# Two unweighted graph layers computed with a dense matrix of edge counts instead of a gather at each edge step

## What is computed

```python
h = relu(_layernorm(x)); x = x + relu(segment_sum((h @ W0)[src] * edge_weight, dst))
h = relu(_layernorm(x)); x = x + relu(segment_sum(norm * (h @ W1.T + b)[src_or_loop], dst_or_loop))
h = relu(_layernorm(x)); x = x + (relu((h + segment_sum(h[src], dst)) @ G1 + g1) @ G2 + g2)
h = relu(_layernorm(x)); x = x + attention over the edges with 8 heads (segment softmax, segment sum)
```

## Time and profile before

| | us |
|---|---|
| three runs | 3065.06, 3089.04, 3067.91; median 3067.91 |
| span of the profiled execution | 3090.3 |
| PE busy, PEld busy | 2381.9 (77%), 1214.8 (39%) |
| DVE, ACT, POOL busy | 1594.0 (52%), 329.1 (11%), 1792.2 (58%) |
| DMA | 557 MB, mean 180 GB/s |
| POOL's gathers of table rows into `ring` | 1721, of some 0.96 us each |

### The profile page before, as it was taken

One profiled execution on the slowest core, in us unless ns is written; L12 is line 12 of the kernel. 1 busy time (PEld: TensorE's weight loads), 2 busy tenths in 40 slices (PEclk: granted clock), 3 DMA queues, 4 the chain that ended last, 5 costly groups with the idle time before them and its releaser, 6 DMA issues.

```text
span 3090.3 us, 32287 instructions
## 1 busy us (share of the span) xinstructions
PE 2381.9 (77%) x8238; PEld 1214.8 (39%) x8238; DVE 1594.0 (52%) x3866; ACT 329.1 (11%) x496; POOL 1792.2 (58%) x1878
## 2 busy tenths in 40 slices
PE   7888888887668777775778888785068598887886
PEld 5444444433223222221344555453058443333332
DVE  8755555644234443323244444444058467777666
ACT  5200000000000000000000000001068200000000
POOL 0466666665566666665666666653710456666665
PEclk9899999998789989887889999997579789999989
DMA  6676666675567766666666666662134457676665
GB/s 161 199 227 175 181 178 179 195 232 164 170 177 212 205 195 209 190 191 183 182 195 198 201 198 199 193 198 69 14 107 146 140 168 206 204 230 191 191 193 163
DMA packets 212803, 557.09 MB, mean 180 GB/s; under 512 B 55477, under 2 KB 56878, under 8 KB 212645
## 3 DMA queue, kind: packets, MB, share of 16 engines
q0 software_dynamic: 144448, 462.60, 52.2%
q1 hardware_dynamic: 67514, 91.15, 9.5%
q10 hardware_dynamic: 683, 1.28, 0.2%
HBM read 515.28 MB, written 39.59 MB: 180 GB/s over the span
## 4 chain that ended last, share of the span: by engine, by line
PE 53%; DVE 13%; issue 13%; another core or an unknown queue 11%; DMA 6%; POOL 3%; ACT 0%; SPq 0%; DVEq 0%; POOLq 0%; ACTq 0%
PE tiles L1520 30%; PE upper L1482 5%; DMA ring<-table,src_t 5%; POOL ring L1855 2%; PE tiles L1517 2%; PE last_bank L1482 2%; PE tiles L1516 2%; PE last_bank L1664 2%; PE upper L1754 1%; DVE sel L812 1%; PE upper L1693 1%; PE upper L1471 1%; POOL ring L1922 1%; DVE ring L1289 1%
## 5 line engine op out<-in xcount | busy, mean ns | idle before, releaser
L1855 POOL DMA_INDIRECT ring<-table,src_t x1320 | 1265.1, 958 | 725.8 <-issue 298.6
L1520 PE MATMUL tiles<-ring,sel 128*125 128x512 f32 x2562 | 1367.7, 661 | 265.4 <-issue 161.1
L1520 PEld LDWEIGHTS tiles<-ring,sel 128*125 128x125 f32 x2562 | 445.3, 200 | 889.0 <-issue 882.6
L1922 POOL DMA_INDIRECT ring<-table,src_t x401 | 385.4, 961 | 229.7 <-PE upper L1524 104.2
L518 DVE TENSOR_TENSOR sel<-iota_bank,dl_t 128x500 f32<-128x500 f32 (+1 forms) x330 | 221.7, 674 | 511.3 <-PE tiles L1520 237.9
L1289 DVE TENSOR_TENSOR ring<-ring,iota_bank 128x512 f32<-128x512 f32 x388 | 255.8, 683 | 113.9 <-DMA ring<-table,src_t 94.1
L1516 PE MATMUL tiles<-ring,sel 128*125 128x512 f16 x440 | 179.9, 409 | 57.1 <-DMA ring<-table,src_t 30.2
L1517 PE MATMUL tiles<-ring,sel 128*125 128x512 f16 x440 | 176.7, 402 | 13.1 <-issue 13.0
L1482 PE MATMUL upper<-wh,hTh 128*125 128x512 f32 x200 | 104.2, 521 | 82.2 <-DVE acc L1024 43.0
L1889 POOL DMA_INDIRECT big<-score_table,src_t x104 | 98.5, 947 | 77.2 <-DMA score_table<-u_all 42.2
L812 DVE TENSOR_SCALAR sel<-node_iota,dl_t,w_t 128x125 f32<-128x125 f32 x440 | 134.8, 359 | 5.8 <-issue 2.9
(11 more groups left out here) (361 smaller groups left out, 2654.2 us busy)
## 6 DMA issues: line engine op xcount, KB each, us to landing
ring<-table,src_t POOLq DMA_INDIRECT x1721
table<-stage SPq DMA_DIRECT2D x50, 224.0 KB
table<-acc SPq DMA_DIRECT2D x50, 224.0 KB
acc<-dst_places SPq DMA_DIRECT2D x28, 256.0 KB
x<-dst_places SPq DMA_DIRECT2D x27, 256.0 KB
x<-in_x SPq DMA_DIRECT2D x25, 224.0 KB
kept_x<-x SPq DMA_DIRECT2D x25, 224.0 KB
x<-kept_x SPq DMA_DIRECT2D x25, 224.0 KB
```

The source lines that it names most:

```text
L1520: last = P.matmul(to, sel[:, n % SELS, :], rows, start=False, stop=True, skip_group_check=True)
L1855: G.indirect_dma_start(out=(ring16 if layer == 2 else ring)[:, n % RING, :], out_offset=None, in_=table[layer][:, :], in_offset=bass.Indir ...
L1922: G.indirect_dma_start(out=rows_at(i), out_offset=None, in_=table[3][:, :], in_offset=bass.IndirectOffsetOnAxis(ap=src_t[:, i:i + 1], axis ...
```

## The change

Layers 1 and 2 no longer gather at each step. Layer 0 and layer 3 keep their 440 steps.

**Tables, beside layer 0.** Each tile of 125 targets is cut into 5 groups of 25 nodes. ACT counts the edges below each group's border (124 passes over the targets with Sign and an accumulated sum), PE sums the counts, DVE works out 540 group steps (`group_tables`) and a key and a low digit for each edge (`edge_keys`), and POOL reads five more blocks of edge rows. DVE also writes layer 1's rows as two float16 halves in place (`z_halves`, three operations for one), and no table is stored.

**The build, after layer 0.** For each of the 540 group steps DVE makes two float16 one-hot matrices, 125 wide (source within its tile) and 650 wide (source's tile and target within the group), and PE adds their product as two matmuls of 325 columns into a pair of PSUM banks. Two pairs take turns. When a group ends, ACT copies 650 columns to SBUF as float16 and clears the pair. When a tile's five groups are there, SP stores its 125x3125 counts (781 KB) to DRAM; ACT waits for the store of three tiles before.

**The dense layers.** For each of 25 tiles PE multiplies 25 blocks of 125x125 counts with the 25 tiles of rows, once for each float16 half: 50 matmuls of 512 columns, 1250 a layer. Counts come back through four slots (`load_counts`), and DVE adds the identity for the node itself (`add_self`). In layer 1 tiles 22 to 24 are computed together, and layer 2's rows, which had been parked in DRAM, come back in place of those that are used up. In layer 2 the dense work of the former lags stands between seven pieces of each tile's 50 matmuls (`BLOCKS`, `LAGS`). Its instructions are those of before.

The core of the diff:

```diff
+            def step_hots(j):
+
+                if j >= HOTS:
+                    V.wait_ge(built, j - HOTS + 1)
+                V.tensor_scalar(out=low_hot[j % HOTS], in0=low_names, scalar1=low_t[:, j:j + 1], scalar2=None, op0=ALU.is_equal).then_inc(hot_ok, 1)
+                V.tensor_scalar(out=key_hot[j % HOTS], in0=key_names, scalar1=key_t[:, j:j + 1], scalar2=None, op0=ALU.is_equal).then_inc(hot_ok, 1)
...
+            def z_halves(k):
+
+                V.wait_ge(pj_out, TILES + k + 1)
+                rows = tmp_z[k % 2]
+                own.mark(V.tensor_scalar(out=rows, in0=acc[0:TN, k, :], scalar1=dis[:, k:k + 1], scalar2=None, op0=ALU.mult))
+                V.wait_ge(v_own, own.n)
+                own.mark(V.tensor_copy(acc16[0:TN, k, 0:D], rows))
+                V.wait_ge(v_own, own.n)
+                V.tensor_tensor(acc16[0:TN, k, D:2 * D], rows, acc16[0:TN, k, 0:D], ALU.subtract).then_inc(halves, 1)
...
+            for k in range(TILES):
+                second_rows(k)
+                add_self(k + SLOTS)
+                next(beside_flags, None)
...
+            def take_groups():
+
+                A.wait_ge(group_steps, 1)
+                for n in range(GROUPS):
+                    t, q = divmod(n, GT)
+                    if q == 0:
+                        A.reg_load(end_regs[0:GT], group_end[0:1, n:n + GT])
+                        if t >= MAKES:
+                            wait_stored(A, COUNTS_N + t - MAKES)
...
+                    A.wait_ge(built, end)
+                    pair = made_bank((n + 1) % 2)[0:TN]
+                    A.copy(made16[t % MAKES][0:TN, :, :, q * GW_N:(q + 1) * GW_N], pair.rearrange("p h (s r) -> p h s r", r=GW_N)).then_inc(taken, 1)
+                    if n + 2 >= GROUPS:
+                        continue
+                    A.wait_ge(taken, n + 1)
+                    A.activation(pair, ident[0:TN, 0:1, None].to_broadcast([TN, 2, HALF_W]), ACT.Copy, scale=0.0).then_inc(room, 1)
...
+            for j in range(BSTEPS):
+                if j % LOADED_TILES == 0:
+                    P.reg_load(tile_regs, group_row[0:1, j:j + LOADED_TILES])
...
+                v = nc.s_assert_within(P.snap(tile_regs[j % LOADED_TILES]) & 127, 1, GROUPS,
+                                       skip_runtime_bounds_check_because="a count of 1 to GROUPS comparisons")
+                P.wait_ge(hot_ok, 2 * (j + 1))
+                P.wait_ge(room, v)
+                for h in range(2):
+                    to = banks[0:TN, bass.ds((v & 1) * 2 + h, 1), 0:HALF_W].rearrange("p a d -> p (a d)")
+                    last = P.matmul(to, low_hot[j % HOTS], key_hot[j % HOTS][:, h * HALF_W:(h + 1) * HALF_W],
+                                    start=False, stop=True, skip_group_check=True)
+                last.then_inc(built, 1)
+
+
+            def dense(n, to, s0, s1):
+                for s in range(s0, s1):
+                    for half in range(2):
+                        last = P.matmul(to[0:TN, :], counts_at(n, s), acc16[0:TN, s, half * D:(half + 1) * D],
+                                        start=(s == half == 0), stop=(s == TILES - 1 and half == 1))
+                return last
...
+            for u in range(TILES * BLOCKS + LAGS[-1][0] + 1):
+                for lag, item in LAGS:
+                    k, at = divmod(u - lag, BLOCKS)
+                    if at == 0 and 0 <= k < (TILES - LATE if item == "rows" else TILES):
+                        works[item](k)
+                k, at = divmod(u, BLOCKS)
+                if k < JOINT:
+                    if at == 0:
+                        second_sums(k, PASSED, TILES)
+                elif k < TILES:
+                    second_sums(k, BLOCK_ENDS[at - 1] if at else 0, BLOCK_ENDS[at])
```

More of the change, by code:

```diff
@@ L68, in build @@
     NB = 4
+    BLOCKS = 7
+    BLOCK_ENDS = [TILES * (b + 1) // BLOCKS for b in range(BLOCKS)]
+    LAGS = ((8, "turned"), (10, "first"), (12, "turned_y"), (14, "second"), (18, "turned_h"), (20, "scores"), (23, "rows"))
     SCORES_FROM = (13, 23, 34)
@@ L1622, in tensor_program @@
-            for i in range(STEPS):
-                step(1, i)
-                flag_rows(i)
+                if (i - TURN_KEYS_AT + 8) % 3 == 0 and 0 <= (i - TURN_KEYS_AT + 8) // 3 < BRB:
+                    turn_key_rows((i - TURN_KEYS_AT + 8) // 3)
+            P.wait_ge(kept, TILES)
+            P.wait_ge(keys_ok, BRB + 1)
+            for pair in (1, 0):
+                P.matmul(bank[2 * pair][0:TN, 0:HALF_W], zeros, wide[:, 0:HALF_W], start=True, stop=True)
+                P.matmul(bank[2 * pair + 1][0:TN, 0:HALF_W], zeros, wide[:, 0:HALF_W], start=True, stop=True).then_inc(room, 1)
@@ L1695, in rows_product @@
                 made["rows"] += 1
-            for i in range(STEPS):
-                step(2, i)
-                for lag, work in ((6, turn_sums), (13, first_product), (27, turn_first), (34, second_product), (48, turn_last),
-                                    (55, score_product), (Z_AT, rows_product)):
-                    k = ended.get(i - lag)
-                    if k is not None:
-                        work(k)
-            score_product(TILES - 4)
-            turn_first(TILES - 2)
-            turn_sums(TILES - 1)
@@ L1709, in tensor_program @@
-            first_product(TILES - 1)
-            second_product(TILES - 2)
-            turn_first(TILES - 1)
-            turn_last(TILES - 3)
-            second_product(TILES - 1)
-            score_product(TILES - 3)
-            turn_last(TILES - 2)
-            rows_product(TILES - 4)
-            turn_last(TILES - 1)
-            score_product(TILES - 2)
-            score_product(TILES - 1)
-            for k in range(TILES - 3, TILES):
+            works = {"turned": turn_sums, "first": first_product, "turned_y": turn_first, "second": second_product,
+                     "turned_h": turn_last, "scores": score_product, "rows": rows_product}
@@ L1721, in tensor_program @@
+            for k in range(TILES - LATE, TILES):
                 rows_product(k)
@@ L1875, in gpsimd_program @@
             G.wait_ge(rows_turned, 1)
[L1876 to L1879 removed]
+            for n in range(TILES - 3, TILES):
+                wait_stored(G, TABLE_N + n)
+            gather_first()
             for q in range(2):
```

1002 lines of the change are left out of this document (681 added, 321 removed).

## The result

The changed kernel takes 3037.98 us (median of 4, 3035.48 to 3040.34) beside 3066.48 (median of 4, 3057.32 to 3089.04) of the kernel before: a ratio of 0.9896, interval 0.9854 to 0.9939. It is faster by 1%, where I had forecast 4% and a range of 2885 to 3015. The range missed the time by 23 us.

The account below looks back on a forecast made before the run. Landing of gathered rows was taken as the bound. Terms 3 + 349 + 8 + 274 + 3 + 563 + 26 = 1226 us replace 1352, 126 less than 3090.3; scaled to the median, 2943 us, range 2885 to 3015.

Parts of the forecast that it names:

- This last stretch and layer 3 are not changed: From layer 2's last node score to the end: taken as equal, 970 us; over 10 us off fails the prediction.
- cost nothing: Layer 0's steps: gathers hide the added ACT work (75 us) and DVE work (some 70 us).
- 22.5 us a tile: Layer 2: PE bounds each tile, 11.8 us dense work with 10.8 of counts; 563 us for 25 tiles.
- rival 2: Dense layers run below full clock rate, some 90 us more, 3035; misread waits in layer 2 cost the same. Chance 0.14.
- The rate of the dense layers: Dense layer 1: matmuls of 512 columns at 0.2155 us each, 1250 of them 269 us.
- The build: 540 steps after layer 0: PE's sequencer sets the pace at 0.646 us a step, 349 us (to 373).
- rival 1: Build: DVE, not PE's sequencer, sets the pace; 266 to 314 us, time 2860 to 2908. Chance 0.10.
- rival 4: Build: ACT's copy-and-clear round trip sets the pace; at 4.5 us per group 563 us, time 3157. Chance 0.05.
- Rival 3: Build: issue costs PE's sequencer 0.07 us more per step, 38 us in all, time 2980. Chance 0.06.
- the rule of 62 ns: Trainium skill's sequencer cost per matmul, rejected for the build; would add some 0.06 us a step, 32 us, time 2975.
- the likeliest case: The forecast itself, chance 0.65: build 325 to 373, dense layers 0 to 40 over, ends 10 either way; 2905 to 3010.
- The steps are bound by the landing of gathered rows: Kernel before, layers 0 to 2: gathered rows' landing, not an engine, sets the 1.475 us step.

Follow-up runs that it names:

- after_again: The changed kernel, unedited, run again beside the kernel before at 3094 us: 3057.0 us, ratio 0.987.
- both_mended: The changed kernel without the mask in the edge scores' target steps and with layer 2's identity addition four pieces later: 2993.9 us, ratio 0.967.
- before_masks: The kernel before with masks on PE's tile numbers in all layers' steps and the edge scores, and on ACT's step counts: 2635.9 us, ratio 1.016.
- second group: Follow-up runs on a chip of their own, where the kernel before takes 3094 us (10 runs).

## Why the prediction was wrong, by its steps

- **"This last stretch and layer 3 are not changed": the largest failure, 34 us.** The edge scores grew by 44 us, and layer 3 was 10 shorter in this execution (612.5, where `after_again` and `both_mended` have 621 and 623). The prediction had named this very check, 970 us and not over 10 off. It also described the edge scores as 148 us in which the engines mostly wait; PE's work on them, 1591 matmuls, lies in the 212 us from the last small gather on. The step that failed is that I priced the new register operations at the build's steps alone and did not follow `step_tile` to its third caller. The earlier trace rows are rows of just this place: they show nine matmuls in 0.65 us with three fused operations. By my own 0.09 us for a plain operation, a mask and a move for each of 440 steps would have been 40 to 80 us. Runs on both kinds of chip show 34 to 44.
- **Layer 0 "cost nothing": 20.9 us.** Two errors. I held the mean load of DVE against layer 3's (425 of 586 us, still true), where the tables' work comes in 50 steps in which DVE is 91% busy. And I read POOL's 0.96 us as its whole cost per gather, where 1.25 passes from one to the next; so five more reads cost about 6.5 us. Shown: the places of the loss, and on the faster chip 9.8 and 6.3 us in them. Some 3 us are the later start of the first step (122.5 for 119.3); in the other runs of the changed kernel and its variants it lies between 117.8 and 123.0, so this is at least in part scatter. That DVE's fullness makes the 9 us of the first 50 steps is argued from its rows: on the slower chips its work there was only added to, and on the faster one spreading it gained 1.7 us there (73.5 to 71.8).
- **Layer 2: 22.5 us a tile was right as a floor, 17 us were on top.** "DVE's `new_rows` and `split_sums` are ready 2 us ahead": I followed the arithmetic and left out `add_self`, a wait of DVE for a DMA, with `new_rows` queued behind it. It is rival 2's last sentence (waits at the pieces), which had, with the rest of rival 2, 0.14. With the addition moved each tile takes 22.57 us.
- **The rate of the dense layers: right.** 10.79 us per 50 matmuls against 10.8 forecast (276.4 us for 276.5), at a granted clock of 0.99. The rest of rival 2 is out.
- **The build: the right bound, and a total that is partly luck.** 352.7 us for 349. One operation more costs 0.083 us (0.09 forecast), one fused operation with its matmul 0.139 in a step that nothing holds (0.13 forecast). A third comparison on DVE costs 3 us of the 92 that it would if DVE set the pace, so rival 1 is out. ACT's pair of 0.72 us each is hidden but for some single waits, so rival 4 is out. Rival 3 would have been 38 us more and is out as well. But two errors cancel: the median step without a load takes 0.545 us, not 0.57 (13 us less over 540), and some 20 us of longer steps, at which PE's idle time is put down to DVE (28 us in 30 times, the usual gap included) and ACT (12 us in 8), had no term at all. (In the passage on the rule of 62 ns, the 0.11 us for an operation without its matmul follows from no term; 0.13 less 0.06 is 0.07, and the nine matmuls with three operations 0.77, still over the 0.65 of the earlier trace rows.)
- **The baseline: 22 us.** I made the sum against an execution of 3090.3 us and took its whole distance to the median off the changed kernel. Before's runs spread over 32 us and after's over 5: perhaps it is the gathering that varies, of which the change takes away half, but no run shows this. Where in before's slow execution its 22 us lie can't be seen either, as only that one was profiled beside the result. And the bounds of the likeliest case add up to 3017 (24, 40 and 10 us on 2943), not to 3010, which is over the range's own end.
- **"The steps are bound by the landing of gathered rows": not borne out, and here lies the most.** On one chip a step took POOL's own pace, 1.27 us, and the gain of 108 us in the replaced stretch became a loss of at least 64. On the first chip PE and POOL halt at irregular places. It is not the mean round trip, since 7 slots do as well as 11, and PE's waits for gathered rows are not longer there (45 us in layer 1, 56 on the faster chip); idle time without a seen event is (538 for 403 us). What halts them stays open. None of my rivals had this case: the slower one was ACT's round trip, which did not happen.

## What to carry to other kernels

When a helper that many loops call gets one more instruction, go through its callers and price it at the one that nothing hides; a stretch with one small matmul per call is where it shows. When work is laid beside a loop, hold it against the busiest fifty steps and against the distance between two starts, not against a mean and a busy time. And when an engine waits for a transfer in order, ask what is queued behind that wait. Here a change that trades gathers for compute moved from a cost that differed by 15% between two chips to one that differed by 0.03%: a gain measured on one chip is no promise for another. When a sum comes out right, compare its terms with the median of single steps too, and not only the total.

## What the runs showed of the hardware

- A plain register operation on PE's sequencer lasts 32 ns in the rows and costs 0.083 us on the average when the sequencer is the bound, 0.097 in a step that nothing else holds; a fused operation with its 325-column matmul 0.139 in such a step. In the edge scores a move and a plain operation together cost 0.08 to 0.10 us per step (34 to 44 us for 440).
- The steps of the kernel before ran at 222 to 228 GB/s on one chip (`before_masks`) and at 191 to 196 on others, with POOL's instruction at 0.95 us on both. Build and dense layers agreed to 0.4 us in 1244.
- While POOL issued small gathers 1.25 us apart, PE ran 990 matmuls in 141 us on that chip and 101 in 135 us on the first one, and a DMA issue of SP lasted 0.34 and 0.70 us.
- The granted clock was lower where PE had less to do: in the build with one matmul of two it was 0.51 for the whole stretch, with both 0.87; in the small gathers, with PE busy 28 of 135 us, 0.56. In the edge scores it was 0.83 with the masks and 0.88 without on the first chip, but 0.86 and 0.87 on the second group's, where the mask cost 35 us all the same.
